# Second expert layer: single tiles first, the largest expert last, four tiles added straight into the output

## The reference

```python
logits = xf @ wr + br                               # 2640 rows, 4 experts
topk_vals, topk_idx = jax.lax.top_k(logits, 2)
gates = jax.nn.softmax(topk_vals, axis=-1)
h = gelu(einsum('nd,edh->enh', xf, w1) + b1)        # 256 -> 1024, exact gelu
y = einsum('enh,ehd->end', h, w2) + b2
c = einsum('eh,ehd->ed', gelu(b1), w2) + b2
out = einsum('nk,nkd->nd', gates, y_sel - c_sel + c.sum(axis=0))
return x + out                                      # x: the layer's input, after attention
```

## Time and profile before

| | |
|---|---|
| median of the runs | 763.83 us |
| the profiled execution's own time | 760.22 us |
| its span, first to last instruction | 758.4 us |
| TensorE busy | 685.8 us, 90% |
| VectorE busy | 452.8 us, 60% |
| ScalarE busy | 378.7 us, 50% |
| GpSimd busy | 285.6 us, 38% |
| mean granted TensorE clock | 0.970 |
| chain that ended last | TensorE 72%, VectorE 12%, ScalarE 8%, DMA 3% |

### The profile page before, as it was taken

One profiled execution on the slowest core, in us unless ns is written; L12 is line 12 of the kernel. 1 busy time (PEld: TensorE's weight loads), 2 busy tenths in 40 slices (PEclk: granted clock), 3 DMA queues, 4 the chain that ended last, 5 costly groups with the idle time before them and its releaser, 6 DMA issues.

```text
span 758.4 us, 18510 instructions
## 1 busy us (share of the span) xinstructions
PE 685.8 (90%) x6176; PEld 599.6 (79%) x6177; DVE 452.8 (60%) x1216; ACT 378.7 (50%) x891; POOL 285.6 (38%) x269
## 2 busy tenths in 40 slices
PE   5989975999999999988799977699999999999981
PEld 5769955988888987667699966688888888888871
DVE  5898787454444444349889868755555454545440
ACT  6899454533434433345599848143443344343440
POOL 3301202124322223126577720235655565565431
PEclk9999997999999999999899999899999999999996
DMA  9996996414221113124644498113323322332235
GB/s 276 231 189 71 134 131 218 139 29 126 39 40 28 29 23 42 15 66 138 135 82 58 57 116 304 29 36 58 46 45 49 56 42 44 54 56 35 37 36 156
DMA packets 42183, 66.24 MB, mean 87 GB/s; under 512 B 3648, under 2 KB 29232, under 8 KB 41584
## 3 DMA queue, kind: packets, MB, share of 16 engines
q0 software_dynamic: 22272, 39.19, 34.0%
q1 hardware_dynamic: 19664, 25.93, 10.6%
q10 hardware_dynamic: 192, 0.38, 0.1%
HBM read 65.80 MB, written 23.35 MB: 118 GB/s over the span
## 4 chain that ended last, share of the span: by engine, by line
PE 72%; DVE 12%; ACT 8%; DMA 3%; issue 2%; POOL 1%; POOLq 0%; DVEq 0%; SPq 0%
PE PS L1165 16%; PE PS L1178 16%; PE PS L872 14%; PE PS L909 8%; PE PS L887 3%; PE PS L1529 2%; PE PS L2533 2%; PE PS L2519 2%; ACT Y L2237 2%; DMA Y<-in_w_dram 1%; PE PS L1150 1%; PE PS L1539 1%; PE PS L1562 1%; PE PS L1584 1%; DMA xs<-Y 1%
## 5 line engine op out<-in xcount | busy, mean ns | idle before, releaser
L1178 PE MATMUL PS<-X 128*128 x720 | 125.7, 273 | 1.9 <-ACT X L1247 1.9
L1336 POOL DMA_INDIRECT sum<-X,dest x45 | 89.2, 1982 | 96.3 <-ACT X L1247 81.1
L1165 PE MATMUL PS<-X 128*128 128x256 f16 (+1 forms) x768 | 122.7, 265 | 2.5 <-DVE X L1267 1.9
L1237 ACT ACTIVATE X<-PS,X 128x256 f32<-128x256 f32 (+1 forms) x192 | 72.8, 463 | 103.6 <-PE PS L1165 100.5
L872 PE MATMUL PS<-Y,X 128*128 128x256 f16 x960 | 108.1, 273 | 0.5 <-DVE Y L1041 0.5
L872 PEld LDWEIGHTS PS<-Y,X 128*128 x960 | 93.8, 98 | 11.6 <-issue 0.7
L1165 PE MATMUL PS<-X,Y 128*128 128x256 f16 (+1 forms) x384 | 100.2, 264 | 0.0
L1178 PE MATMUL PS<-Y,X 128*128 x360 | 98.2, 273 | 0.0
L1136 POOL DMA_INDIRECT sum<-Y,dest x24 | 39.7, 1656 | 111.5 <-DVE Y L1069 107.9
L1165 PEld LDWEIGHTS PS<-X 128*128 x768 | 71.7, 97 | 12.6 <-issue 3.1
L1178 PEld LDWEIGHTS PS<-X 128*128 128x128 f16 x720 | 70.4, 98 | 10.7 <-issue 2.6
(11 more groups left out here) (410 smaller groups left out, 1351.5 us busy)
## 6 DMA issues: line engine op xcount, KB each, us to landing
X<-in_w_dram POOLq DMA_DIRECT2D x16, 1024.0 KB, 11.5
sum<-h SPq DMA_DIRECT2D x2, 2048.0 KB, 10.0
Y<-in_w_dram POOLq DMA_DIRECT2D x4, 1024.0 KB, 11.7
xs<-Y SPq DMA_DIRECT2D x2, 1040.0 KB, 5.2
xs<-Y SPq DMA_DIRECT2D x2, 1032.0 KB, 5.3
h<-in_txt_dram SPq DMA_DIRECT2D x2, 1024.0 KB, 16.3
Y<-in_patches_dram SPq DMA_DIRECT2D x3, 672.0 KB, 7.5
sum<-h SPq DMA_DIRECT2D x2, 768.0 KB, 11.6
```

Of the source, the lines that this page charges most:

```text
L1165: ins = nc.tensor.matmul(PS[:, 2 * s + c // 2, (c % 2) * T1:(c % 2) * T1 + tokens], part[:, off:off + P], x_[:, slot, k, 0:tokens], start= ...
L1178: ins = nc.tensor.matmul(PS[:, 4 + a, 0:D], h_[:, s, c, a * P:(a + 1) * P], part[:, off:off + D], start=(s == 0 and c == 0 and n == 0), st ...
L1237: ins = nc.scalar.activation(hh1[:, s, c, 0:tokens], PS[:, 2 * s + c // 2, (c % 2) * T1:(c % 2) * T1 + tokens], ACT.Gelu, bias=bias1[:, sl ...
L1336: nc.gpsimd.indirect_dma_start(out=sum1, out_offset=bass.IndirectOffsetOnAxis(ap=dest[:, i:i + 1], axis=0), in_=y1buf[:, u % 2, i - first_ ...
```

## The change

The order of the list is turned round: the three single tiles are units 0 to 2, pairs follow, and the expert with most rows comes last, so that the last four tiles hold only rows of one expert. `positions` gets two forms: `in_order`, as before, for the first expert layer, and `taken_first` with `experts_in_turn` for the second. The places are counted from the end (`k_back`).

No row is twice in the last four tiles, and they hold no empty places. They are added straight into `out`: `straight` turns their places in `sum1` into places in `out`. SP waits for the sends of the first 41 tiles only, then copies `sum1` to `out`, all four DMAs on its queue. GpSimd sends tile 41 once that copy has landed. Each send still waits for the sends of the unit before.

The steps are written out for the first six units and the last two, with a loop for the others (`pipelined1`). The first 12 bias products leave attention's last step and stand with the others. `rest_of_outputs` moves behind the split of unit 1's rows in VectorE's first step; `straight` stands in its step 3.

```diff
+body(i, i % 2, i // 2)
+
+
+def pipelined1(eng, n, body):
+
+    for i in range(6):
+body(i, i % 2, i // 2)
+    with eng.Fori(3, (n - 2) // 2) as j:
+body(2 * j, 0, j)
+body(2 * j + 1, 1, j)
+    for i in range(n - 2, n):
 body(i, i % 2, i // 2)
...
-def summed(eng):
+def summed(eng, tiles):
-        eng.wait_ge(y1_out[k], 16 * uses_of(k, TILES1))
+        eng.wait_ge(y1_out[k], 16 * uses_of(k, tiles))
...
-    store_image(sp, 0)
+    for i in range(PER):
+        store_image(sp, i)
+    summed(sp, TILES1)
...
-    return isinstance(i, int) and i >= PAIRS1
+    return isinstance(i, int) and i < SINGLES1
-    return PAIRS1 + i if is_single(i) else 2 * i
+    return i if is_single(i) else 2 * i - SINGLES1
-    return t // 2 if t < 2 * PAIRS1 else t - PAIRS1
+    return t if t < SINGLES1 else (t + SINGLES1) // 2
-    return t % 4 if t < 2 * PAIRS1 else 2 * (unit_of(t) % 2)
+    return 2 * (unit_of(t) % 2) + t - first_tile(unit_of(t))
-    return 16 * len([t for t in range(first_tile(i) + 1) if unit_of(t) % 2 == slot]) if is_single(i) else 32 * (j + 1)
+    return 16 * (i // 2 + 1) if is_single(i) else 32 * j + 16 * slot
...
+def taken_first(chain, upto, so):
+
+    n_of = upto[:, :, NT - 1:NT].broadcast_to([P, 4, NFULL])
+    tl, st, odd = raf[:, 176:184], raf[:, 184:188], raf[:, 192:200]
+    pairs_to, odd_to, keep = raf[:, 200:208], raf[:, 208:216], raf[:, 224:232]
+    rank, top = raf[:, 216:220], raf[:, 220:221]
+    chain.link(nc.vector.scalar_tensor_tensor(out=rank.unsqueeze(2), in0=upto[:, :, NT - 1:NT], scalar=4.0,
+                                              in1=k_slot[:, 0:4].unsqueeze(2), op0=ALU.mult, op1=ALU.add))
+    for a in range(2):
+        full = raf[:, 4 * a * NFULL:4 * (a + 1) * NFULL].rearrange("p (g k) -> p g k", g=4)
+        ins = nc.vector.tensor_tensor(full, n_of, k_fill[:, :, :], ALU.is_gt)
+    chain.link(ins)
+    chain.link(nc.vector.tensor_reduce(top, rank, AX, ALU.max))
+    full = raf[:, 0:8 * NFULL].rearrange("p (g k) -> p g k", g=8)
+    chain.link(nc.vector.tensor_reduce(tl, full[:, :, 1:NFULL:2], AX, ALU.add))
+    chain.link(nc.vector.tensor_reduce(odd, full[:, :, 0:NFULL:2], AX, ALU.add))
+    for a in range(2):
+        ins = nc.vector.tensor_scalar(keep[:, 4 * a:4 * a + 4], rank, top, None, ALU.is_lt)
+    chain.link(ins)
+    chain.link(nc.vector.tensor_tensor_scan(pairs_to, keep, tl, 0.0, ALU.mult, ALU.add))
+    chain.link(nc.vector.tensor_tensor(odd, odd, tl, ALU.subtract))
+    chain.link(nc.vector.tensor_tensor(st, pairs_to[:, 4:8], tl[:, 4:8], ALU.subtract))
+    chain.link(nc.vector.tensor_tensor_scan(odd_to, keep, odd, 0.0, ALU.mult, ALU.add))
+    chain.link(nc.vector.tensor_scalar(sm[:, 8:16], raf[:, 180:188], float(T1), None, ALU.mult))
+    chain.link(nc.vector.tensor_tensor(so, odd_to[:, 4:8], odd[:, 4:8], ALU.subtract))
+    return st
+
+def experts_in_turn(chain, st, so, sf, sg_, tiles, singles):
+
+    keep, before_first, first = raf[:, 224:228], raf[:, 236:240], raf[:, 232:233]
+    chain.link(nc.vector.scalar_tensor_tensor(out=before_first, in0=keep, scalar=-1.0, in1=k_slot[:, 0:4], op0=ALU.add,
+                                              op1=ALU.mult))
+    chain.link(nc.vector.tensor_reduce(first, before_first, AX, ALU.add))
+    for g in range(1, 4):
+        chain.link(nc.vector.scalar_tensor_tensor(out=sf, in0=k_slot[:, 0:tiles], scalar=st[:, g:g + 1],
+                                                  in1=sf, op0=ALU.is_le, op1=ALU.add))
+    chain.link(nc.vector.tensor_scalar(sg_, k_slot[:, 0:singles], so[:, 0:1], None, ALU.is_ge))
+    for g in range(1, 4):
+        chain.link(nc.vector.scalar_tensor_tensor(out=sg_, in0=k_slot[:, 0:singles], scalar=so[:, g:g + 1],
+                                                  in1=sg_, op0=ALU.is_ge, op1=ALU.add))
+    chain.link(nc.vector.tensor_tensor(sf[:, 0:singles], sf[:, 0:singles], sg_, ALU.min))
+    chain.link(nc.vector.tensor_scalar(sf, sf, first, 1.0, ALU.subtract, ALU.subtract))
+    over_ = tok[:, 2, 0:tiles]
+    chain.link(nc.vector.tensor_scalar(over_, sf, 4.0, -4.0, ALU.is_ge, ALU.mult))
+    nc.vector.tensor_tensor(slote[:, 0:tiles], sf, over_, ALU.add).then_inc(slots_ready, 1)
+
+def straight(dve, chain):
+
+    ends = slice(TILES1 - STRAIGHT, TILES1)
+    tile_, token = raf[:, 240:244], tok[:, 1, ends]
+    row, part, image, text = (raf[:, 244 + 4 * i:248 + 4 * i] for i in range(4))
+    both = lambda out_, a, x, b, op0, op1: chain.link(
+        nc.vector.scalar_tensor_tensor(out=out_, in0=a, scalar=float(x), in1=b, op0=op0, op1=op1))
+    both(text, tile_, IMG, token, ALU.mult, ALU.add)
+    both(row, tile_, -P, token, ALU.mult, ALU.add)
+    chain.link(nc.vector.tensor_scalar(part, row, float(IMG), None, ALU.is_ge))
+    both(part, row, 2 * IMG, part, ALU.is_ge, ALU.add)
+    both(image, tile_, PER * SEQ, row, ALU.mult, ALU.add)
+    both(image, part, SEQ - IMG, image, ALU.mult, ALU.add)
+    both(image, image, BATCH * PER * SEQ + IMG, text, ALU.subtract, ALU.subtract)
+    both(image, tile_, BATCH, image, ALU.is_ge, ALU.mult)
+    both(dest[:, ends], image, IMG, text, ALU.add, ALU.add)
+    dve.sem_inc(dest_ready, 1)
 
 def positions(dve, chain, choices, tiles, done, inrow, intile, pairs, singles):
 
...
+    st = taken_first(chain, upto, so) if done else in_order(chain, upto, odd, so)
...
+    if done:
+        chain.link(nc.vector.tensor_tensor(pos[:, 0:choices, :], k_back[:, :].unsqueeze(1).broadcast_to([P, choices, NT]),
+                                           slots_of, ALU.subtract))
+    else:
+        chain.link(nc.vector.tensor_tensor(pos[:, 0:choices, :], slots_of,
+                                           k_far.unsqueeze(1).broadcast_to([P, choices, NT]), ALU.add))
...
+    if done:
+        chain.link(nc.vector.tensor_scalar(st, st, -2.0, float(TILES1 - 1), ALU.mult, ALU.add))
+        chain.link(nc.vector.tensor_scalar(sf, k_slot[:, 0:tiles], st[:, 0:1], None, ALU.is_le))
+    else:
...
+    if done:
+        chain.link(nc.vector.tensor_copy(raf[:, 240:244], tile_[:, TILES1 - STRAIGHT:TILES1]))
+    if done:
+        experts_in_turn(chain, st, so, sf, sg_, tiles, singles)
+        return
...
-            if not (isinstance(j, int) and j == 0):
-                act.wait_ge(y1_out[2 * slot + a], 16 * j)
+            uses = j if a == 0 else j - (1 if slot else 2)
+            if not (isinstance(uses, int) and uses <= 0):
+                act.wait_ge(y1_out[2 * slot + a], 16 * uses)
...
-def dve_experts1(dve, chain):
+def dve_experts1(dve, chain, rest):
...
             dve_scale(dve, chain, 1)
         if not known(i, UNITS1 - 1):
             split_x(i + 1, 1 - slot, j + slot, expert_of(i + 1))
+        if known(i, 0):
+            rest()
+        if known(i, 3):
+            straight(dve, chain)
         split_h(i, 0)
         if not known(i, 0):
             base_y(i - 1, expert_of(i - 1))
         split_h(i, 1)
-    pipelined(dve, UNITS1, tile, 2)
+    pipelined1(dve, UNITS1, tile)
     base_y(UNITS1 - 1, expert_of(UNITS1 - 1))
 
 def pool_slots1(pool):
...
             for before in range(first_tile(u - 1), i):
                 pool.wait_ge(y1_out[buffer_of(before)], 16 * uses_of(buffer_of(before), before + 1))
         pool.wait_ge(y1_copied, i + 1)
+        if i == TILES1 - STRAIGHT:
+            pool.wait_ge(dest_ready, 3)
+            pool.wait_ge(out_written, 16 * (1 + PER))
         nc.gpsimd.indirect_dma_start(
-            out=sum1, out_offset=bass.IndirectOffsetOnAxis(ap=dest[:, i:i + 1], axis=0),
+            out=sum1 if i < TILES1 - STRAIGHT else out.rearrange("b s d -> (b s) d"), out_offset=bass.IndirectOffsetOnAxis(ap=dest[:, i:i + 1], axis=0),
             in_=y1buf[:, u % 2, i - first_tile(u), :], in_offset=None, compute_op=ALU.add)\
             .then_inc(y1_out[buffer_of(i)], 16)
     pool_slots(pool, TILES1, 8, gather, send)
...
         if b % PER == PER - 1:
             image_values(b // PER + 1)
     heads(pe, batch)
-    pe.wait_ge(gb_split, 1)
-    pe.wait_ge(*w1_whole(0))
-    bias_out(pe, 0, range(0, F1 // P // 2))
     transpose_p(BATCH - 1)
     values(BATCH - 1, (BATCH - 1) % 2)
 
...
-    summed(sp)
+    summed(sp, TILES1 - STRAIGHT)
...
-    summed(act)
-    for i in range(1, PER):
-        store_image(nc.scalar, i)
...
-    bias_out(pe, 0, range(F1 // P // 2, F1 // P))
-    for e in range(1, E1):
+    pe.wait_ge(gb_split, 1)
+    for e in range(E1):
         bias_out(pe, e)
...
-    rest_of_outputs()
-    dve_experts1(dve, chain)
+    dve_experts1(dve, chain, rest_of_outputs)
...
+    nc.gpsimd.tensor_scalar(k_back[:, :], k_far, float(P * TILES1 - 1), None, ALU.add)
```

More of the change, by code:

```diff
@@ L696, in dest_of_token, with in_order @@
             chain.link(nc.vector.tensor_tensor(to, to, from_, ALU.add))
+        def in_order(chain, upto, odd, so):
+            n_of = upto[:, :, NT - 1:NT].broadcast_to([P, 4, NFULL])
+            full = raf[:, 0:4 * NFULL].rearrange("p (g k) -> p g k", g=4)
```

(31 more changed lines are left out.)

13 lines of the change are left out of this document (2 added, 11 removed).

## The result

The changed kernel takes 768.09 us (median of 7 runs, 766.36 to 770.66), the kernel before beside it 764.56 (763.34 to 766.37): ratio 1.0043, 95% interval 1.0025 to 1.0061. It is slower, and the time lies outside the range of 760.9 to 766.3. The ratio compares with executions of the kernel before that were measured beside it. Run again later as a control, unedited, it gave 1.0067 (1.0046 to 1.0087). So experiments are best compared within one batch, which is a set of kernels measured side by side on one chip. A difference is given by the ratios; where the medians say something else, that is said too.

A forecast was written before the change was run, and what follows sets the result against it. TensorE's own time was taken to bound the layer, so only its ends could move: start -1.16, layer and end -1.05 in all without the clock, clock +0.9, span 758.25, so 763.7 us; range 760.9 to 766.3.

The forecast's parts named there:

- part 5: The kernel's end: copy hidden, four ordered sends behind it, last landed at 756.9, span ending 0.45 later at 757.35.
- The copy: SP's copy of sum1 to the output near the end: 10.2 us as before, from 733.8 to 744.0.
- the rival of +1.1: At the end, the copy takes longer with all four DMAs on one queue: +1.1, 764.8 us; chance 0.08.
- part 6: TensorE's clock falling in the wait for the scale product: 0.9 taken, between no fall and one, bounds 0 and 3.4.
- a double fall: Rival: TensorE's clock falls waiting for the scale product and for unit 0's split: 3.4, 766.2 us; chance 0.22.
- part 4: Singles first: a wait of 2.1 for unit 0's split, then steps of units 1 to 3 of 4.4, 6.56 and 8.32.
- the 1.3 and 2.0 of the longer routing: VectorE's added routing operations: +1.3 for computing places ahead of the gather, +2.0 for the list of experts by tile.
- the singles' first blocks: First-layer product blocks of the single tiles on TensorE: 2.0 each for the first three, 1.75 for the next three.
- the four ordered sends: GpSimd's sends of tiles 41 to 44 behind the copy, in two groups 6.4 apart: 12.8 us.
- part 1: Attention's last step without the 12 bias products: routing starts 2.3 earlier, the products covered later.
- no change: Whole kernel: -0.15 in span, 763.7 us, no measurable change; forecast chance 0.38, same time 0.40.

The follow-up runs named there:

- e1_early_copy: The kernel before with its copy of the sums made before the second layer's first send, so the output lacks the experts' part: 758.82 us, ratio 0.9920.
- e1_dummies: The changed kernel with 75 instead of 40 dummy products behind the slot map: 765.83 us, ratio 1.0006.
- e3_control: The changed kernel itself, unedited, measured again in a later batch against the kernel before: ratio 1.0067.
- e1_order_only: The changed kernel with no straight tiles, all 45 added into sum1 and the copy behind all sends: 767.13 us, ratio 1.0028.
- e4_best: The changed kernel with eight straight tiles, no landing waits between straight units, and 75 dummies instead of 40: ratio 0.9924.

## Why the prediction was wrong

Forecast 758.25 in span time, measured 766.3. By its own steps, the difference of 8.05:

| step | forecast | measured | difference |
|---|---|---|---|
| ahead of the change (the anchor) | 441.03 | 442.24 | +1.21 |
| anchor to first product, with 0.9 for the clock | 49.62 | 49.49 | -0.13 |
| first product to the pair's second send (unit 21) | 239.70 | 241.93 | +2.23 |
| second send to SP's copy | 4.35 | 3.95 | -0.40 |
| SP's copy to the send of tile 41 | 10.35 | 12.07 | +1.72 |
| four sends, first to last | 8.40 | 8.46 | +0.06 |
| last send to the end of the span | 4.80 | 8.16 | +3.36 |

**The step that failed** is the end of part 5: "landed for SP at 756.9; 0.45 to the end of the span as before". The 0.45 was carried over from a kernel whose last event was a copy on SP. There the drain of GpSimd's queue had long ended; here a send is last, and the drain ends 4.0 after that send is seen landed. That is +3.2 to +3.4 in all fourteen profiles and most of the 4.4 by which the medians miss. e1_early_copy shows it apart from all else. The trace of before held the row; a look at the end of every engine's queue would have found it.

**The copy** was mis-sized next. From SP's first issue to GpSimd's next send it took 12.07 and not 10.35. The chain of waits parts this, from SP's last issue to that send:

```profile
739.58 9.22 DMA out_dram<-sum
748.80 0.02 issue
748.83 0.04 POOLq L1440
748.87 0.81 issue
```

The copy was seen landed at 748.80, 11.19 after SP's first issue at 737.61 and not 10.2. GpSimd's send began 0.88 later and not 0.15; these 0.7 stand in all seven profiles with four straight tiles. The landing varies there from 10.4 (e1_dummies) to 11.5 (e3_control). In e1_order_only, where nothing else runs beside the copy and all four DMAs stand on SP's queue too, it is 10.5. So the one queue, the rival of +1.1, is worth about 0.3, and the rest of the term varies by execution.

**The clock** (part 6): 0.9 stood for no fall or one. The places and the kind of a double fall were right as a rival, its size of 3.4 too large. The dummies, which take away both, gave 2.8 (between batches) and 2.6 (within one) by the ratios, 2.2 in stretches B and C. So 0.9 was 1.3 to 1.9 short. The first fall hid in a sum that came out right by chance. The way to the scale product was 1.6 longer and not 3.3, because of something that I hadn't forecast. Before, the slot map's 44 products took 5.22 at 1.2 GHz behind an idle gap of 4.01. Now the dummies ahead of them start later and, at 1.2 GHz themselves, end later; the gap is 1.46, and the map runs at full clock (2.30 and 0.79). What the change lost to one fall it gained by the absence of another.

**The first units** are most of the +2.23 between the first product and unit 21's second send. From unit 0's second products (500.39) to unit 3's first products (512.75) it took 12.36, and part 4 had 4.4 + 6.56 = 10.96: 1.4 more. Unit 3's step took 8.32 and the later ones 10.93, as forecast. The other 0.8 is the first send of the pair, 2.52 long, which delays the second. The second fall shows in those 12.36: the 12 second products behind the wait took 2.53, and 1.33 in e1_dummies. Yet e1_dummies, at full clock, needs 12.15 for the same way, because its blocks of products take up to 1.99 and TensorE waits ahead of two of them. So what was mis-sized is the pace of the steps of units 1 and 2, by 1.2 without any fall, and of the second fall only 0.2 is left at unit 3.

**What was right:** the 1.3 and 2.0 of the longer routing (places +1.4, list of experts +2.1 in the trace); the first products to the second products of unit 0, 8.66 against 8.68, with a wait of 1.83 that I had at 2.1 (in part by luck, since 0.3 of it is the slow clock: 8.37 in e1_dummies); the singles' first blocks; the four ordered sends, two groups apart; the gain of part 1, where the clock holds; a copy that TensorE's work covers nearly to its end. The chances put "no change" first, since the unforeseen 3.4 was in no case.

Not settled: what sets A's clock fall from one execution to the next, and whether the biases cost more in the changed kernel (2.2 to 3.0) than in the kernel before (1.7 to 1.9).

## What to carry to other kernels

When a change alters which engine finishes last, list the last instruction of every queue, the drains too, and cost the new last one by itself: a term that was hidden is not zero. Work that is moved beside other work pays only if its new end lies before that of its cover; with four straight tiles the first send behind the copy began 2.3 after the last copy of results had begun (749.68 against 747.36), and eight turned a loss of 0.4% into a gain of 0.4%. Compare traces from an anchor ahead of the edit, and medians only within a batch.

## What was new about the hardware

- A kernel whose last DMA is one of GpSimd's indirect sends ends 8.0 to 8.2 after that send's issue begins: some 4 until the landing is seen, and 4.0 more of DRAIN on GpSimd's queue. The send's own row shows 1.56. The Trainium skill, Perfetto Trace Analysis, "DMA Instruction — SWDGE (GPSIMD)", says that such a row ends when the descriptors are made and not when the data has moved; the trace agrees with it. The drain behind the landing no row of that instruction shows.
- The length of an idle time alone doesn't say whether TensorE keeps 2.4 GHz. It held over idle times of 2.42, 2.51 and 2.73 (e1_dummies, e4_best). It was lost 2.5 into an idle time in the kernel before (the prediction read 2.45), 3.3 into the 4.37, but only 1.1 into the 1.94 ahead of the 50 dummies. It also fell in attention's last step, where no single wait was over 0.82.
- Removing waiting work can cost clock. With the 12 bias products in attention's last step the clock held there in two of three profiles (not in e1_early_copy), without them in four of fourteen. That it was their work that kept it is likely and not shown by itself.
